# Remainders of the routed experts' second matrices: made once during attention, kept in DRAM, and loaded per block

## The reference

```python
h = concat(patch_embed(x), txt)                       # 32 x 69 x 256
h = h + softmax_attention(layernorm(h))               # 16 heads of 16
h = h + moe_1(layernorm(h))                           # 8 experts of 128, 2 chosen, and a shared one
h = h + linear_attention_block(layernorm(h))          # with its own feed-forward of 1024
for e in range(8):                                    # moe_2, C = 256, hidden 1024, 2 of 8 chosen
    hid = new_gelu(x_flat @ w1[e].T + b1[e])
    out_e = hid @ w2[e].T + b2[e]
    output = output + cw[:, e:e + 1] * out_e
h = h + output
```

## Time and profile before

| | us |
|---|---|
| median of 3 runs | 1312.89 |
| the profiled execution, its own time | 1315.2 |
| its span in the trace | 1313.4 |
| attention, about | 112 to 324 |
| routed experts, about | 963 to 1280 |
| PE, DVE, POOL, ACT busy, share of the span | 80%, 65%, 51%, 39% |

### The profile page before, as it was taken

One profiled execution on the slowest core, in us unless ns is written; L12 is line 12 of the kernel. 1 busy time (PEld: TensorE's weight loads), 2 busy tenths in 40 slices (PEclk: granted clock), 3 DMA queues, 4 the chain that ended last, 5 costly groups with the idle time before them and its releaser, 6 DMA issues. The chain is left out here.

```text
span 1313.4 us, 23693 instructions
## 1 busy us (share of the span) xinstructions
PE 1049.5 (80%) x7608; PEld 928.4 (71%) x7608; DVE 857.8 (65%) x1522; ACT 513.1 (39%) x1014; POOL 676.3 (51%) x631
## 2 busy tenths in 40 slices
PE   7277999998739999578888577888159999999980
PEld 6255777777738988456666577778149999999980
DVE  1445555554656667659999323333659999999994
ACT  0101444444112222243434344446136566666650
POOL 1046444441345445324343655556038999999970
PEclk9688999997759999788888688889569999999995
DMA  7630000000000000000000600002511111111105
GB/s 253 210 133 1 0 0 0 0 0 0 0 0 1 0 0 0 0 1 0 0 0 0 263 1 12 13 13 67 226 54 35 38 36 36 36 40 36 36 28 211
DMA packets 21444, 58.49 MB, mean 45 GB/s; under 512 B 4713, under 2 KB 12338, under 8 KB 20066
## 3 DMA queue, kind: packets, MB, share of 16 engines
q1 hardware_dynamic: 12418, 35.20, 7.2%
q0 software_dynamic: 4848, 14.72, 3.5%
q10 hardware_dynamic: 4144, 8.16, 1.7%
HBM read 46.73 MB, written 13.57 MB: 46 GB/s over the span
## 5 line engine op out<-in xcount | busy, mean ns | idle before, releaser
L1913 DVE TENSOR_TENSOR place<-place,place 128x1024 fp32r<-128x1024 f32 x85 | 197.1, 2318 | 2.9
L121 DVE CAST place<-place 128x512 fp32r<-128x512 f32 (+6 forms) x263 | 136.0, 548 | 62.6 <-ACT place L1025 38.8
L1877 PE MATMUL moe_up<-place,place 128*128 128x128 f32 x1376 | 162.6, 277 | 0.0
L1877 PEld LDWEIGHTS moe_up<-place,place 128*128 128x128 f32 x1376 | 159.2, 194 | 0.0
L127 PE MATMUL moe_down<-place,place 128*128 128x256 f32 x1008 | 142.2, 291 | 10.2 <-DVE place L1913 7.7
L127 PEld LDWEIGHTS moe_down<-place,place 128*128 128x128 f32 x1008 | 126.2, 191 | 18.7 <-DVE place L1913 18.7
L1851 POOL TENSOR_TENSOR place<-place,place 128x512 fp32r<-128x512 f32 x84 | 123.3, 1468 | 13.3 <-DVE place L121 11.5
L1949 ACT ACTIVATE place<-moe_up,place 128x128 f32<-128x128 f32 x344 | 97.5, 366 | 24.1 <-POOL place L1851 23.7
L1936 ACT ACTIVATE place<-place 128x2048 f32 x44 | 84.0, 1912 | 43.7 <-PEq L1688 29.9
L1830 POOL DMA_INDIRECT place<-xn_rows,place x44 | 74.8, 1699 | 49.5 <-POOLq L1688 39.1
L1045 POOL TENSOR_TENSOR place<-place,place 128x384 fp32r<-128x384 f32 x57 | 58.3, 1023 | 79.0 <-DVE place L121 79.0
(11 more groups left out here) (233 smaller groups left out, 2161.4 us busy)
## 6 DMA issues: line engine op xcount, KB each, us to landing
place<-in_w_dram SPq DMA_DIRECT2D x4, 4096.0 KB, 13.3
place<-choices ACTq DMA_DIRECT2D x5, 768.0 KB, 7.1
place<-in_patches_dram SPq DMA_DIRECT2D x9, 384.0 KB, 3.8
place<-in_e_dram SPq DMA_DIRECT2D x2, 1152.0 KB, 7.5
xn_rows<-place SPq DMA_DIRECT2D x6, 384.0 KB, 2.4
place<-in_f_dram SPq DMA_DIRECT2D x2, 1024.0 KB, 11.7
out_dram<-place SPq DMA_DIRECT2D x5, 384.0 KB, 4.9
place<-stream POOLq DMA_DIRECT2D x2, 768.0 KB, 5.1
```

What stands on the lines that cost most here:

```text
L121: return eng.tensor_copy(out, x)
L1877: last = pe.matmul(p1[u][k // HK][:, (k % HK) * P:(k % HK + 1) * P], ws[u][:, c, k * P:(k + 1) * P], xT[u][:, c, :], start=(c == 0), stop= ...
L1913: dve.tensor_tensor(w2_lo[f], w2, w2_hi[f].bitcast(F32), ALU.subtract).then_inc(w2_split, 1)
```

## The change

During attention the remainders of all 8 experts' w2 are made in 16 parts of 128x1024 (half an expert each, W2 = 16). For each part SP loads it from DRAM, ACT makes the leading part in a scratch tile (`cut_w2`), POOL subtracts (`make_rest`, in place), and SP stores the remainder in a DRAM tensor `w2_rest`. Two parts are handled ahead of the loops, the other 14 in the loops, one after every second step: POOL's `make_rest(j)` stands behind POOL step n, and ACT's cut of j behind ACT step n, for n = 1, 3, 5, ..., 27 and j = 2 to 15.

In the routed experts DVE keeps the leading part of w2 and no longer makes the remainder. SP instead reads the owner of the next block and loads the remainders from `w2_rest` in four quarters of 256 KB (2 KB for each partition), each as soon as the six matmuls that read the quarter before are done (`quarter_mm`). PE waits for each quarter (`w2_rest_in`).

```diff
@@ attention @@
+        m.at(self.w1_at)
+        w2_raw, w2_rest = zip(*[m.both(KF // 2, D) for _ in range(2)])
+        w2_lead = m.take_rounded(KF // 2, D)
+        W2 = 2 * E
             @block.sync
             def _(sp):
                 sp.wait_ge(self.rest_in, 16 * self.rest_count)
+                for j in range(2):
+                    sp.dma_start(w2_raw[j], self.t["w2"][:, j * rows:(j + 1) * rows, :]).then_inc(w2_part_in[j], 16)
+                for j in range(W2):
+                    sp.wait_ge(w2_rest_made, j + 1)
+                    sp.dma_start(self.w2_rest[:, j * rows:(j + 1) * rows, :], w2_rest[j % 2].bitcast(F32)).then_inc(w2_rest_out[j % 2], 16)
+                    if j + 2 < W2:
+                        sp.wait_ge(w2_rest_out[j % 2], 16 * (j // 2 + 1))
+                        sp.dma_start(w2_raw[j % 2], self.t["w2"][:, (j + 2) * rows:(j + 3) * rows, :]).then_inc(w2_part_in[j % 2], 16)
             def _(pool):
+                def make_rest(j, u):
+                    pool.wait_ge(w2_cut, j + 1)
+                    pool.tensor_tensor(w2_rest[u], w2_raw[u], w2_lead.bitcast(F32), ALU.subtract).then_inc(w2_rest_made, 1)
                 stage_qk(0, 0) ... stage_x(1, 1)
-                with pool.Fori(0, NB // 2 - 1) as i:
-                    for u in range(2):
-                        n = i * 2 + u
+                make_rest(0, 0)
+                make_rest(1, 1)
+                with pool.Fori(0, NB // 4 - 1) as i:
+                    for u in range(4):
+                        n = i * 4 + u
                         pool.wait_ge(s_mm, n + 1)
+                        stage_qk(n + 2, u % 2)
                         pool.wait_ge(v_mm, n + 1)
+                        stage_x(n + 2, u % 2)
+                        if u % 2 == 1:
+                            make_rest(i * 2 + (2 + u // 2), u // 2)
             def _(act):
+                def cut_w2(j, u):
+                    act.wait_ge(w2_part_in[u], j // 2 * 16 + 16)
+                    act.wait_ge(w2_rest_made, j)
+                    act.activation(w2_lead, w2_raw[u], ACT.Copy).then_inc(w2_cut, 1)
                 copy_v(0, 0)
                 copy_v(1, 1)
                 exp(0, 0)
+                cut_w2(0, 0)
+                cut_w2(1, 1)
+                with act.Fori(0, NB // 4 - 1) as i:
+                    for u in range(4):
+                        step_of(i * 4 + u, i * 2 + u // 2, u % 2, True, True)
+                        if u % 2 == 1:
+                            act.wait_ge(w2_part_in[u // 2], i * 16 + 32)
+                            act.wait_ge(w2_rest_made, i * 2 + (2 + u // 2))
+                            act.activation(w2_lead, w2_raw[u // 2], ACT.Copy).then_inc(w2_cut, 1)
@@ routed @@
             def _(sp):
+                def load_rest(e, q):
+                    sp.dma_start(w2_lo[q // 2][:, (q % 2) * 2:(q % 2) * 2 + 2, :].bitcast(F32),
+                                 self.w2_rest[:, bass.ds(e * KF + q * 2, 2), :]).then_inc(w2_rest_in[q], 16)
+                e = owner_of(sp, 0)
+                for q in range(4):
+                    load_rest(e, q)
+                with sp.Fori(0, NBLK) as n:
+                    e = owner_of(sp, n + 1)
+                    for q in range(4):
+                        sp.wait_ge(quarter_mm[q], n + 1)
+                        load_rest(e, q)
             def _(pe):
-                            pe.wait_ge(w2_split, n * 2 + f + 1)
+                            pe.wait_ge(w2_cut, n * 2 + f + 1)
                             for k in range(HK):
+                                q = f * 2 + k // 2
+                                if k % 2 == 0:
+                                    pe.wait_ge(w2_rest_in[q], n * 16 + 16)
                                 last = product(...)
+                                if k % 2 == 1:
+                                    last.then_inc(quarter_mm[q], 1)
             def split(n, f, e):
-                    dve.wait_ge(w2_cut, n * 2 + f + 1)
-                    dve.tensor_tensor(w2_lo[f], w2, w2_hi[f].bitcast(F32), ALU.subtract).then_inc(w2_split, 1)
```

More of the change, by code:

```diff
@@ L643, in attention @@
         pt = m.take(4, H2, S)
+        m.at(self.w1_at)
+        w2_raw, w2_rest = zip(*[m.both(KF // 2, D) for _ in range(2)])
+        w2_lead = m.take_rounded(KF // 2, D)
+        W2 = 2 * E
+        self.w2_rest = self.dram("w2_remainder", [P, E * KF, D])
+        w2_part_in, w2_cut, w2_rest_made, w2_rest_out = sem("w2_part_in", 2), sem("w2_part_cut"), sem("w2_rest_made"), sem("w2_rest_out", 2)
         staged, keyed = sem("x_staged"), sem("qk_staged")
@@ L662, in _ @@
                 sp.wait_ge(self.rest_in, 16 * self.rest_count)
+                rows = KF // 2
+                for j in range(2):
[6 more added lines that the diff above has]
+                        sp.dma_start(w2_raw[j % 2], self.t["w2"][:, (j + 2) * rows:(j + 3) * rows, :]).then_inc(w2_part_in[j % 2], 16)
+                for j in range(2):
+                    sp.wait_ge(w2_rest_out[j], 16 * (W2 // 2))
             @block.gpsimd
             def _(pool):
+                def make_rest(j, u):
+                    pool.wait_ge(w2_cut, j + 1)
+                    pool.tensor_tensor(w2_rest[u], w2_raw[u], w2_lead.bitcast(F32), ALU.subtract).then_inc(w2_rest_made, 1)
                 def stage_x(n, u):
@@ L678, in _ @@
                 stage_x(1, 1)
-                with pool.Fori(0, NB // 2 - 1) as i:
-                    for u in range(2):
-                        n = i * 2 + u
+                make_rest(0, 0)
[3 more added lines that the diff above has]
+                        n = i * 4 + u
                         pool.wait_ge(s_mm, n + 1)
-                        stage_qk(n + 2, u)
+                        stage_qk(n + 2, u % 2)
                         pool.wait_ge(v_mm, n + 1)
-                        stage_x(n + 2, u)
+                        stage_x(n + 2, u % 2)
+                        if u % 2 == 1:
+                            make_rest(i * 2 + (2 + u // 2), u // 2)
+                for u in range(2):
+                    n = NB - 4 + u
+                    pool.wait_ge(s_mm, n + 1)
+                    stage_qk(n + 2, u)
+                    pool.wait_ge(v_mm, n + 1)
+                    stage_x(n + 2, u)
             @block.tensor
@@ L811, in _ @@
                 exp(0, 0)
-                with act.Fori(0, NB // 2 - 1) as i:
-                    for u in range(2):
-                        step_of(i * 2 + u, i, u, True, True)
+                cut_w2(0, 0)
[7 more added lines that the diff above has]
+                            act.activation(w2_lead, w2_raw[u // 2], ACT.Copy).then_inc(w2_cut, 1)
+                for u in range(2):
+                    step_of(NB - 4 + u, NB // 2 - 2, u, True, True)
                 step_of(NB - 2, NB // 2 - 1, 0, True, False)
@@ L1801, in routed @@
         ws_ready, up_mm, gl = sem("moe_w1_staged"), sem("moe_up_mm"), sem("moe_gelu", 2)
-        h_cut, h_split, w2_cut, w2_split = sem("moe_hidden_cut"), sem("moe_hidden_split"), sem("moe_w2_cut"), sem("moe_w2_split")
-        half_mm, down_mm, y_read, stored = sem("moe_half_mm"), sem("moe_down_mm", 2), sem("moe_down_read"), sem("choices_stored", 2)
+        h_cut, h_split, w2_cut, w2_rest_in = sem("moe_hidden_cut"), sem("moe_hidden_split"), sem("moe_w2_cut"), sem("moe_w2_rest_in", 4)
+        quarter_mm, y_read, stored = sem("moe_quarter_mm", 4), sem("moe_down_read"), sem("choices_stored", 2)
         self.choices = self.dram("choices", [1 + 2 * NT * P, D])
@@ L1822, in _ @@
                 sp.dma_start(w1_b, t["w1_b"]).then_inc(b_in, 16)
+                def load_rest(e, q):
[9 more added lines that the diff above has]
+                        load_rest(e, q)
+                for q in range(4):
+                    sp.wait_ge(w2_rest_in[q], 16 * (NBLK + 1))
             @block.gpsimd
@@ L1892, in _ @@
                             pe.wait_ge(h_split, split_count(n, f))
-                            pe.wait_ge(w2_split, n * 2 + f + 1)
+                            pe.wait_ge(w2_cut, n * 2 + f + 1)
                             for k in range(HK):
+                                q = f * 2 + k // 2
+                                if k % 2 == 0:
+                                    pe.wait_ge(w2_rest_in[q], n * 16 + 16)
                                 last = product(pe, p2[:, 0:D], (hi[f][:, k, :], lo[f][:, k, :]), (w2_hi[f][:, k, :], w2_lo[f][:, k, :]),
                                                f + k == 0, f == 1 and k == HK - 1)
-                            if f == 0:
-                                last.then_inc(half_mm, 1)
-                        last.then_inc(down_mm[u], 1)
+                                if k % 2 == 1:
+                                    last.then_inc(quarter_mm[q], 1)
             @block.vector
@@ L1919, in _ @@
                         e, following = owner_of(dve, n), owner_of(dve, n + 1)
-                        dve.wait_ge(down_mm[1 - u], i + u)
```

(7 more changed lines are left out.)

## The result

| | median, us | runs |
|---|---|---|
| before | 1313.64 | 4 (1311.35 to 1316.03) |
| after | 1416.84 | 4 (1415.38 to 1418.78) |

The ratio is 1.0786, 95% interval 1.0762 to 1.0811: the change made the kernel slower, by 103 us. The forecast was 1391, in a range of 1350 to 1425. The profiled execution took 1416.42 us (span 1414.6), 101.2 more than the one of before, and the difference lies in two stages with opposite signs.

The account below looks back on a forecast made before the run. PE was taken to bound attention, and DVE the routed experts. The sum 1315.2 + 8.1 + 2 + 49 + 35 - 16 = 1393.3, with the profiled execution 2.3 above the median, gave 1391 us, range 1350 to 1425.

Parts of the forecast that it names:

- POOL's wait behind its odd step delays x of a later sequence: Attention loop: POOL's subtraction waits for ACT's cut, so PE's values start 3.5 us late, 14 times, 49 us in all.
- The sign given for POOL: Attention trace after the change: POOL would stand before `make_rest` for about 9 us each time, released by ACT.
- The start: Start of attention: two cuts and subtractions ahead of POOL step 0 make PE's first values 8.1 us late.
- The clock: Attention: PE's stalls bring the lower clock level, costing 2.5 us per stall, 35 us over 14, and 2 at the start.
- the short case: Attention clock: the lower level lasts some 3.7 us, as after a routed-experts wait, costing 1.7 us per stall.
- the long case: Attention clock: the lower level lasts some 9 us of work, as at attention's end, costing 4.2 us per stall.
- The routed experts: Routed experts: without DVE's subtraction a block goes from 7.11 to 6.77 us; with the first block, 16 us gained.
- The clock holds: Rival, attention: the stall is there but the clock does not fall, 1354 us; chance 0.08.
- POOL stays the bound: Rival, routed experts: POOL keeps its durations and the steady part gains nothing, 1405 us; chance 0.06.
- The quarters come late: Rival, routed experts: remainder loads land in 6.0 us plus 0.5 for issue, block 7.27 us, 1411 in all; chance 0.04.
- The wait costs nothing: Rival, attention: the cut arrives before POOL's next step would have begun, 1297 to 1305 us; chance 0.05.
- The clock stays at the lower level through attention: Rival, attention: two steps of 12.5 us become 23.8 at the lower clock, 1465 us in all; chance 0.03.

Follow-up runs that it names:

- fill_7: The changed kernel with 7 extra matmuls, results never read, on PE ahead of the values of every even attention step: 1353.14 us.
- cut_even: The changed kernel with ACT's cut of each part in the loop moved from behind its odd step to behind the even step before: 1305.67 us.
- spread: The changed kernel with one cut ahead of ACT's loop, the others behind even steps, subtractions behind even POOL steps, none ahead of POOL's loop: 1292.35 us.
- quarters_late: The changed kernel with SP issuing all four remainder loads only after the block's last matmul: 1447.98 us.

## Why the prediction was right, and which term was off

- **POOL's wait behind its odd step delays x of a later sequence.** Right, and right in size: 3.5 us a pair were forecast, 3.23 in the pair shown, and 15.87 - 12.5 = 3.4 where the clock holds; 14 x 3.4 = 48 against 49. The sign given for POOL was off: it stands before `make_rest` for 13.0 us in the mean (181.6 / 14), not 9, since the slow clock stretches the steps in which it waits (8.3 in `fill_7` at 160.67, where the clock holds). The durations that were taken from other lines held: the cut 1.04 us (forecast 1.06), the subtraction 2.34 (2.34). `cut_even` shows the cause: only the order was changed.
- **The start.** Forecast 8.1 and 2 for the clock. The delay came as forecast: the values of PE step 0 start 131.71 - 113.32 = 18.39 us after the first scores, and 124.97 - 114.60 = 10.37 before, 8.0 late. The clock cost more. Up to the scores of PE step 1 the loss is 10.7 us (23.85 against 13.2), and those scores still run at the lower level (3.93 us); up to PE step 2 it is 32.38 - 19.42 = 13.0, so 4.9 for the clock.
- **The clock.** The term that was mis-sized, and the main cause of the 26 us between 1391 and 1416.8: 2.5 us a pair were taken and 4.6 came, 14 x 4.6 = 64 us instead of 35. I had chosen near the short case, because values and scores follow the stall. They do, and the level still stayed down for some 10 us, close to the long case (4.2 was the upper estimate and too low). The choice failed, not the mechanism: `fill_7` takes the term away with useless matmuls.
- **The routed experts.** 21 us instead of 16. Terms: 0.45 a block instead of 0.34, because the twelve matmuls of a half take 1.48 us each time (2.95 for 24) when PE runs through, where I had read 1.53 from a half that followed a wait. The rest is the first block and the last. POOL gave back what was expected of the scatter (2.05 to 1.00), 0.8 of the gather (1.77 to 0.98) where 1.1 was taken, and nothing on its subtraction; per block it is busy 5.3 us instead of 6.7, so there was room for that. The price taken for the quarters, 3.8 us, held: the kernel after has no number for their landing, but in `spread` the same loads land in 3.8 us in the median. The longest took 5.6 of the 6.0 us of cover, so the margin is thin.
- **The sum** by measured terms: 1315.2 + 13.0 + 112.5 - 21.0 = 1419.7, against 1416.4 for the profiled execution. The 112.5 are the 14 pairs from PE step 2 to PE step 30, (433.45 - 145.70) - (309.23 - 134.02), where 48 and 64 make 112. The rest lies outside the terms: attention starts 1.3 us earlier, its last steps are 1.0 shorter, the stages between it and the routed experts 1.5, and the end is 0.5 longer. The errors of the forecast partly cancel: 29 us too little for the clock in the loop and 3 at its start, 5 too little for the gain.
- **The rivals.** "The clock holds" is `fill_7`, 1353 against the 1354 given for it, but it took an edit to get there. "POOL stays the bound" fell: PE is busy 30.00 of 30. "The quarters come late" fell for the change and is real one edit away (`quarters_late`). "The wait costs nothing" fell; its threshold, the cut one step earlier, is `cut_even`, and it gave 1306 where 1297 to 1305 was said. "The clock stays at the lower level through attention" fell: each pair but one came back to 1.00.

## What to carry to other kernels

On an in-order engine ask of an added instruction not only how long it is and whether the engine has idle time, but what it waits for and what stands behind it: here 3.4 us of work per two steps fitted easily, and cost 8 us (3.4 of standing still, 4.6 of slow clock) because the instruction waited for the end of a step that its successor was to feed. Put producer and consumer a full step apart, so that the wait is over when it is reached. And price a new pause of TensorE with the slow stretch that follows: here it cost more (4.6 us) than the pause itself (3.4).

## What the hardware showed

- After a pause of 3.2 us the clock stayed at the lower level through about 10 us of busy TensorE in attention, and in one pair, after 3.13 us, through some 20 (0.50 from 174 to 192), while in the routed experts it was back some 3.7 us after a pause of 1.77.
- Pauses of 1.4 to 1.5 us were followed by the lower level in eight cases of twelve in the same kernel; at 0.2 us all pairs of the loop but one (scores of 3.75 us) ran at full speed. What decides stays open; the length of the pause alone does not.
- A float32 matmul of 128x69 by 256 took 0.43 us, in two records of 0.215.
- Transfers of 196 GB/s in the routed stage left PE at 30.00 busy us of 30 and the block at 6.66 us: they cost nothing that can be seen.
